# A two-layer graph network: the second layer's gathers without a bound on their indices

## The chip, the cores and the metric

The kernel runs on one core of a Trainium2 chip. The metric is the time of one execution on the device in microseconds (us), as the median of several runs. The engines are named as in the profile: PE is the matrix engine (PEld its weight loads), DVE the vector engine, ACT the scalar engine, POOL is GpSimd and SP the engine that issues most plain transfers.

## The reference

There are 6250 nodes with 256 features, and 106250 edges, sorted by their destination, each with one of 8 types. The first layer sums, for each node, the features of its neighbours and multiplies:

```
x = layernorm(x + relu(x @ w0 + segment_sum((x @ w1)[src_of_message], receiver)))
```

The second layer is an attention over the same edges. For each of the 8 types there is a table `h_all[type] = x @ W[type].T` of 256 features, seen as 8 heads of 32:

```
h_src  = h_all[edge_type, src];  h_dst = h_all[edge_type, dst]
scores = leaky(sum(h_src * attn_src) + sum(h_dst * attn_dst))      # per edge and head, slope 0.2
w      = exp(scores - segment_max(scores, dst));  w = w / segment_sum(w, dst)
x      = layernorm(x + segment_sum(h_src * w, dst))
```

The heavy irregular read is `h_all[edge_type, src]`: one row for every edge, out of 8 x 6250 rows.

## The kernel before, in words

The whole kernel is one function, `graph_layers`, with one block of instructions per engine. All order between the engines is written by hand with semaphores: `x.wait_ge(s, n)` holds an engine until semaphore `s` has reached `n`, and `.then_inc(s, k)` adds `k` when an instruction or a transfer is done. A transfer adds 16 to its semaphore.

The edges are cut into 880 steps. A step holds up to 128 edges (one on each partition) of one tile of 128 destination nodes. Sixteen steps are a batch, and there are 55 batches (NB in the code; B is 16).

First layer (lines 975 to 993): POOL scatters the sums of each step into one of four tables in DRAM with an indirect transfer that adds (line 985, 880 of them). Each carries the bound `node_bound`. Its loop over the batches is a loop on the device. Before it, seven indirect transfers at line 968 fetch rows of edges, also with a bound.

Building of the tables: PE makes the 8 products of each tile of nodes, and ACT writes them with the attention terms to `ha_d` in DRAM, 51200 rows of 264 numbers (256 features and 8 terms, one for each head).

Second layer: for batch b, POOL's `gather(b, s)` (lines 1019 to 1027) issues 16 indirect transfers. Each fetches 128 rows of `ha_d`, picked by the 128 indices in one column of `idx_t`, into one of the 16 places of the buffer `rows[s]`. There are four such buffers, s = b mod 4 (they lie in the memory called `region`). A quarter of four gathers is issued once PE has read the same quarter of that buffer four batches before (`g.wait_ge(segs, ...)`, line 1021). The 880 gathers are written out one by one, as is all of the second layer on PE, DVE and ACT; SP runs a loop.

In iteration i of the layer the engines work on three batches at once: they prepare batch i + 1 (PE line 1361, DVE lines 614 and 619, ACT line 1148), they compute the scores and weights of batch i (DVE line 672 is the first to read the gathered rows of a batch; then DVE lines 674 to 736, PE lines 1392, 1400 and 1412), and they sum batch i - 1: DVE's line 624 multiplies the rows by their weights, a quarter at a time, PE's line 1370 (`sum_edges`) sums the edges of each step into PSUM, which also gives the quarter of the buffer back to POOL, and DVE's line 636 adds the sums to the accumulators.

After the last batch the accumulators are divided by the sums of the weights, the residual is added and the rows are normalised and stored.

The bound of the gathers, `row_bound`, is a register that is set once (line 972) to the last row of the table; an index above it would be an error. The indices all lie within the table.

Of the kernel before, what the change touches and what calls it, by code (L numbers as in the profile page):

```python
# [21 lines left out]
def graph_layers(nc, x, xT, src, dst, etype, w0, w1, W, WT, attn_src, attn_dst, out):  # L22
# [18 lines left out]
    B = P // H  # L41
# [29 lines left out]
    with ExitStack() as ctx:  # L71
        def sb(name, shape, dt):
            return ctx.enter_context(nc.sbuf_tensor(name, shape, dt))

        def sem(name):
            return ctx.enter_context(nc.semaphore(name))
# [9 lines left out]
        idx_t = sb("idx_t", [P, KP], I32)  # L86
# [189 lines left out]
        gath = [[sem(f"gath{s}{q}") for q in range(4)] for s in range(4)]  # L276
# [22 lines left out]
        def in_pairs(eng, first, end, body):  # L299

            with eng.Fori(0, (end - first) // 2) as i:
                for n in range(first, first + 2):
                    body(2 * i + n, n % 2, i + n // 2)
            if (end - first) % 2:
                body(end - 1, (end - 1) % 2, (end - 1) // 2)
# [654 lines left out]
        @block.gpsimd  # L960
        def _(g):
            g.iota(it_i, [[1, P]], base=0, channel_multiplier=0).then_inc(iotas, 1)
            g.iota(pt_i, [[0, 1]], base=0, channel_multiplier=1).then_inc(iotas, 1)

            g.wait_ge(setup, SU["tiles"])
            g.wait_ge(rows_stored, 16)
            for b in range(BLK):
                g.indirect_dma_start(step_f[:, b, :], None, edge_rows_d,
                                     bass.IndirectOffsetOnAxis(ap=i_i[:, b:b + 1], axis=0),
                                     bounds_check=KP - 1, oob_is_err=True).then_inc(step_rows, 16)  # L970
            node_bound = g.snap(g.to_reg(NP_ - 1))
            row_bound = g.snap(g.to_reg(NP_ * R - 1))


            def scatter(it):
                for q in range(4):
                    h = q % 2
                    g.wait_ge(sums_copied, 4 * it + q + 3)
                    g.wait_ge(slots_ready, 4 * it + q + 1)
                    for u in range(4):  # L980

                        if not isinstance(it, int) or q:
                            g.wait_ge(scattered[1 - h][u], 16 * (2 * it + (q + 1) // 2))
                        g.sem_inc(pool_turns, 1)
                        g.indirect_dma_start(sums_d[u],  # L985
                                             bass.IndirectOffsetOnAxis(ap=idx_slot[:, 0, 4 * q + u:4 * q + u + 1], axis=0),
                                             sums[h][:, u, :], None, bounds_check=node_bound, oob_is_err=True,
                                             compute_op=ALU.add).then_inc(scattered[h][u], 16)

            g.wait_ge(zeroed, 16 * NACC)  # L990
            scatter(0)
            with g.Fori(1, ITS) as it:
                scatter(it)

            def add_parts(it, par, turns):
                two = parts[par][:, 2:4, :, :]
                g.wait_ge(parts_in[par], 16 * NACC * (turns + 1))
                g.tensor_tensor(two[:, 0, :, :], two[:, 0, :, :], two[:, 1, :, :], ALU.add).then_inc(pooled, 1)  # L1000

            def inverse_deviation(it, par):
                g.wait_ge(veps_made, it + 1)
                g.tensor_tensor(rstd[par][:, :], veps[par][:, :], minus_half[:, :], ALU.pow).then_inc(rstd_made, 1)  # L1004

            def add_and_invert(it, par, turns):
                add_parts(it, par, turns)
                inverse_deviation(it - 1, 1 - par)

            add_parts(0, 0, 0)  # L1010
            in_pairs(g, 1, ITN, add_and_invert)
            inverse_deviation(ITN - 1, (ITN - 1) % 2)


            for h in range(2):
                g.wait_ge(h_stored[h], 16 * (ITN + 1))
            ha_rows = ha_d.rearrange("n (r w) -> (n r) w", w=AW)

            def gather(b, s):
                for q in range(4):  # L1020
                    g.wait_ge(segs, B * b + 4 * q + 4)
                    g.sem_inc(pool_turns, 1)
                    for u in range(4):
                        k = 4 * q + u
                        g.indirect_dma_start(rows[s][:, k, :], None, ha_rows,  # L1025
                                             bass.IndirectOffsetOnAxis(ap=idx_t[:, B * b + k:B * b + k + 1], axis=0),
                                             bounds_check=row_bound, oob_is_err=True).then_inc(gath[s][q], 16)

            g.wait_ge(begun, 1)
            for b in range(NB):  # L1030
                gather(b, b % 4)


            def finish(it, par, turns):
                g.wait_ge(fveps_made, it + 1)
                g.tensor_tensor(rstd[par][:, :], veps[par][:, :], minus_half[:, :], ALU.pow).then_inc(frstd_made, 1)

            in_pairs(g, 0, ITN, finish)
# [400 lines left out]
```

## Time and profile before

| | |
|---|---|
| median of 3 runs | 3920.17 us (3910.32 to 3921.48) |
| profiled execution | 3891.99 us |
| its span | 3890.1 us |
| its mean TensorE clock, share of the full one | 0.758 |
| POOL busy | 2379.8 us, 61% of the span |
| PE busy | 2260.3 us, 58% |
| DVE busy | 1898.7 us, 49% |
| ACT busy | 1099.7 us, 28% |

The busy shares are averages over stages that differ much: POOL is the fullest engine of the first layer, and PE and DVE are the fullest of the second. The profiled execution is one run, and its time lies below the three others. A row of the trace names the engine, the line of the kernel, the instruction and what it writes and reads (`region<-ha_d,idx_t` is a gather). Where it shows idle time before an instruction it names who ended it; "issue" is time in which the profile shows nothing that the engine waited for, and "another core or an unknown queue" (also "remote") a release of which it shows no source.

### The profile page before, as it was taken

What the parts mean: (1) busy time and instruction counts of PE and PEld (TensorE: products, weight loads), DVE (VectorE), ACT (ScalarE), POOL (GpSimd) and SP (SyncE); (2) the same over time, 40 slices, a digit from 0 to 9 for tenths busy, and PEclk for the clock granted to TensorE, in tenths of its full rate; (3) what the DMA queues carried; (4) which work ended last, traced back from release to release, by engine and by line L of the source; (5) the groups of instructions that cost most, each with busy time, mean ns of one, the idle gap of its engine ahead of it and who ended that gap; (6) DMA issues with size and microseconds to landing.
All of it is one profiled execution on the core that took longest, in us unless ns stands there. A gap on an engine that the chain in (4) does not pass through costs nothing.

```text
span 3890.1 us, 43658 instructions
## 1 busy us (share of the span) xinstructions
PE 2260.3 (58%) x8426; PEld 1550.0 (40%) x8427; DVE 1898.7 (49%) x6684; ACT 1099.7 (28%) x2537; POOL 2379.8 (61%) x1848
## 2 busy tenths in 40 slices
PE   5444444444444444444999926777776676777660
PEld 4333333333333333332555514555545444555440
DVE  2433333333333333332333315777776676777677
ACT  2211222122212221221333303344444333444330
POOL 0477888888888888885111065666666665666601
PEclk8766676666666766676999957888888887888875
DMA  9678876777776767677656433333333333333303
GB/s 339 137 99 136 150 88 88 88 88 88 88 89 88 88 87 88 88 88 165 222 217 227 174 110 82 94 92 98 94 93 93 95 93 89 96 96 96 93 23 114
DMA packets 318535, 443.64 MB, mean 114 GB/s; under 512 B 49188, under 2 KB 273642, under 8 KB 311504
## 3 DMA queue, kind: packets, MB, share of 16 engines
q0 software_dynamic: 169520, 236.24, 38.2%
q1 hardware_dynamic: 141696, 152.01, 13.4%
q10 hardware_dynamic: 7200, 54.07, 3.4%
q8 instruction: 43, 0.70, 0.1%
q14 instruction: 76, 0.62, 0.1%
HBM read 216.80 MB, written 218.81 MB: 112 GB/s over the span
## 4 chain that ended last, share of the span: by engine, by line
issue 31%; PE 29%; DMA 19%; DVE 9%; ACT 5%; POOL 4%; DVEq 1%; another core or an unknown queue 1%; POOLq 0%; ACTq 0%; SPq 0%; PEldq 0%
PE ps L1370 12%; DMA sums_d<-edge_z,idx_slot 11%; PE ps L1315 9%; DMA sums_d<-sums,idx_slot 7%; POOL sums_d L985 4%; PE ps L1361 3%; DVE nodes L636 3%; DVE region L624 2%; ACT edge_z L1083 2%; DVE region L614 1%; PE ps L1223 1%; ACT sums L1083 1%; PE ps L1295 1%; ACT region L1159 1%; DVE region L619 1%
## 5 line engine op out<-in xcount | busy, mean ns | idle before, releaser
L1025 POOL DMA_INDIRECT region<-ha_d,idx_t x880 | 920.5, 1046 | 567.6 <-issue 329.3
L1266 PE MATMUL ps<-region,edge_z 128*128 x1760 | 649.6, 533 | 653.6 <-ACT edge_z L1091 642.4
L1370 PE MATMUL ps<-region 128*128 128x264 f32 x1760 | 681.8, 533 | 375.2 <-DVE nodes L636 236.3
L985 POOL DMA_INDIRECT sums_d<-sums,idx_slot x440 | 689.3, 1567 | 240.6 <-issue 109.6
L985 POOL DMA_INDIRECT sums_d<-edge_z,idx_slot x440 | 686.4, 1560 | 143.9 <-issue 120.1
L1266 PEld LDWEIGHTS ps<-region,edge_z 128*128 128x128 f32 x1760 | 455.2, 272 | 774.9 <-issue 688.4
L1370 PEld LDWEIGHTS ps<-region 128*128 128x128 f32 x1760 | 385.4, 248 | 604.4 <-issue 381.3
L439 DVE TENSOR_TENSOR idx_slot<-dup,edge_z 128x4 int32<-128x4 f32 x220 | 35.9, 163 | 968.8 <-DMA sums_d<-edge_z,idx_slot 512.8
L636 DVE TENSOR_TENSOR nodes<-ps,nodes 128x264 f32 x880 | 378.7, 430 | 141.3 <-DVE nodes L636 68.2
L1315 PE MATMUL ps<-region,edge_z 128*128 128x512 f32 x800 | 351.6, 593 | 0.0
L1361 PEld LDWEIGHTS ps<-edge_z,region 128*128 128x128 f32 x1760 | 276.7, 229 | 80.1 <-issue 62.2
L1083 ACT COPY edge_z<-ps 128x1024 f32<-128x1024 f32 x110 | 111.3, 1012 | 693.9 <-DMA sums_d<-edge_z,idx_slot 693.4
L1361 PE MATMUL ps<-edge_z,region 128*128 x1760 | 263.8, 303 | 53.7 <-issue 52.1
L624 DVE TENSOR_TENSOR region<-region 128x1024 f32<-128x1024 f32 x220 | 266.3, 1211 | 58.0 <-issue 56.1
L1083 ACT COPY sums<-ps 128x1024 f32<-128x1024 f32 x110 | 111.3, 1012 | 638.4 <-DMA sums_d<-sums,idx_slot 618.0
L1152 ACT ACTIVATE region<-iota_row,local_t 128x128 f32<-128x128 f32 x880 | 280.6, 395 | 0.0
L1277 PE MATMUL ps<-edge_z 128*128 128x128 bf16 x880 | 117.1, 276 | 279.7 <-DVE edge_z L423 277.6
L1148 ACT ACTIVATE region<-ps 128x512 f32<-128x512 f32 x220 | 129.9, 590 | 329.2 <-PE ps L1351 205.9
L1277 PEld LDWEIGHTS ps<-edge_z 128*128 128x128 bf16 x880 | 82.2, 126 | 352.2 <-DVE edge_z L423 312.9
L1004 POOL TENSOR_TENSOR rstd<-veps,minus_half 128x2 f32<-128x2 f32 x25 | 23.8, 950 | 320.9 <-DVE veps L583 320.9
L1315 PEld LDWEIGHTS ps<-region,edge_z 128*128 128x128 f32 x800 | 148.4, 191 | 167.2 <-issue 167.2
L614 DVE TENSOR_TENSOR region<-ps,region 128x256 f32<-128x256 f32 x220 | 92.9, 422 | 242.4 <-PE ps L1361 143.0
(173 smaller groups left out, 2567.5 us busy)
## 6 DMA issues: line engine op xcount, KB each, us to landing
ha_d<-region ACTq DMA_DIRECT2D x50, 1056.0 KB, 4.0
row<-step_rows_d SPq DMA_DIRECT2D x220, 128.0 KB
sums_d<-sums SPq DMA_DIRECT2D x4, 6400.0 KB, 28.8
region<-sums_d SPq DMA_DIRECT2D x100, 256.0 KB, 3.7
region<-ha_d,idx_t POOLq DMA_INDIRECT x880
edge_z<-level_d SPq DMA_DIRECT2D x55, 136.0 KB
kl_d<-nodes SPq DMA_DIRECT2D x8, 903.0 KB
edge_z<-kl_d SPq DMA_DIRECT2D x55, 129.0 KB
```

The costliest lines, as they stand in the source:

```text
L614: v.tensor_tensor(prod[q % 2], ps[:, 5 + q % 2, 0:4 * RH] .rearrange("p (u h r) -> p u h r", u=4, h=H), tmask[s % 2][:, 4 * q:4 * q + 4, : ...
L624: v.tensor_tensor(rows[s][:, 4 * q:4 * q + 4, 0:D].rearrange("p u (h d) -> p u h d", h=H), rows[s][:, 4 * q:4 * q + 4, 0:D].rearrange("p u ...
L636: v.tensor_tensor(acc[:, ds(tile[u] * AW, AW)], ps[:, u, 0:AW], acc[:, ds(tile[u] * AW, AW)], ALU.add).then_inc(added, 1)
L985: g.indirect_dma_start(sums_d[u], bass.IndirectOffsetOnAxis(ap=idx_slot[:, 0, 4 * q + u:4 * q + u + 1], axis=0), sums[h][:, u, :], None, b ...
L1025: g.indirect_dma_start(rows[s][:, k, :], None, ha_rows, bass.IndirectOffsetOnAxis(ap=idx_t[:, B * b + k:B * b + k + 1], axis=0), bounds_ch ...
L1083: a.copy(sums[h][:, :, :], ps[:, 2 + 2 * h:4 + 2 * h, :].rearrange("p b (u n) -> p (b u) n", u=2)).then_inc(sums_copied, 1)
L1152: last = a.activation(apart[q % 2][:, u, :], iota_row[:, :], ACT.Abs, bias=local_t[:, ds(B * b + 4 * q + u, 1)], scale=-1.0)
L1266: mm = t.matmul(ps[:, 2 + 2 * h + u // 2, (u % 2) * D:(u % 2) * D + D], lhsT=counts[h][:, u, :], rhs=y_sb[:, ds(tile[4 * q + u] * D, D)], ...
L1277: mm = t.matmul(ps[:, h, u * P:(u + 1) * P], lhsT=onehot[h][:, u, :], rhs=eq[h][:, u, :], start=True, stop=True)
L1315: mm = t.matmul(ps[:, 4 + q, :], lhsT=xts[par][:, h, c, :], rhs=wT_sb[:, c, 512 * q:512 * q + 512], start=(c == 0), stop=(c == DC - 1))
L1361: mm = t.matmul(ps[:, 5 + q % 2, RH * u:RH * u + RH], lhsT=st[q % 2][:, u, :], rhs=b_sb[:, ds(tile[4 * q + u] * RH, RH)], start=True, stop ...
L1370: t.matmul(ps[:, u, 0:AW], lhsT=sel[q][:, u, :], rhs=rows[s][:, 4 * q + u, :], start=True, stop=True).then_inc(segs, 1)
```

## The change

The gathers of the second layer lose two arguments, the bound and what is to happen beyond it. The scatters of the first layer and the transfers of line 968 keep theirs. The register `row_bound` is still set, and nothing reads it.

```
                         g.indirect_dma_start(rows[s][:, k, :], None, ha_rows,
-                                             bass.IndirectOffsetOnAxis(ap=idx_t[:, B * b + k:B * b + k + 1], axis=0),
-                                             bounds_check=row_bound, oob_is_err=True).then_inc(gath[s][q], 16)
+                                             bass.IndirectOffsetOnAxis(ap=idx_t[:, B * b + k:B * b + k + 1],
+                                                                       axis=0)).then_inc(gath[s][q], 16)
```

## Rows read from the trace of the kernel before

**Rows 1.** Busy us (instructions) of PE, PEld, DVE, ACT, POOL; then clock, DMA share, GB/s.

```profile
2350.00:3800.00 1450.00, 1010.13 (x4099) 716.61 (x4099) 1039.34 (x2714) 574.49 (x1626) 858.99 (x821) 0.82 0.34 89
```

**Rows 2.** The chain that ended last, its shares by line.

```profile
PE ps L1370 12%; DMA sums_d<-edge_z,idx_slot 11%; PE ps L1315 9%; DMA sums_d<-sums,idx_slot 7%; POOL sums_d L985 4%; PE ps L1361 3%; DVE nodes L636 3%; DVE region L624 2%; ACT edge_z L1083 2%; DVE region L614 1%; PE ps L1223 1%; ACT sums L1083 1%; PE ps L1295 1%; ACT region L1159 1%; DVE region L619 1%
```

**Rows 3.** Line 1025: busy, mean ns, idle before; ns min/median/max; who waited for it.

```profile
L1025 POOL DMA_INDIRECT region<-ha_d,idx_t x880 | 920.5, 1046 | 567.6 <-issue 329.3 <-PE ps L1370 226.9 <-remote 11.4
...
L1025 POOL DMA_INDIRECT region<-ha_d,idx_t x880: 1006/1012/2055, 2257.7 to 3692.9; - x176
...
  DVE region L672: 8.3, 1
```

**Rows 4.** Line 1025 in two stretches: ns min/median/max, first and last start.

```profile
L1025 POOL DMA_INDIRECT region<-ha_d,idx_t x64: 1007/1012/1133, 2257.7 to 2340.9; - x64
...
L1025 POOL DMA_INDIRECT region<-ha_d,idx_t x272: 1006/1012/2008, 2355.7 to 2797.4; - x136
```

**Rows 5.** DVE's line 672, once a batch: start us, us.

```profile
2351.27 0.28 DVE L672 TENSOR_TENSOR region<-region 128x128 f32<-128x128 f32 x1
...
2800.26 0.28 DVE L672 TENSOR_TENSOR region<-region 128x128 f32<-128x128 f32 x1
...
3639.95 0.28 DVE L672 TENSOR_TENSOR region<-region 128x128 f32<-128x128 f32 x1
3665.64 0.28 DVE L672 TENSOR_TENSOR region<-region 128x128 f32<-128x128 f32 x1
3694.92 0.29 DVE L672 TENSOR_TENSOR region<-region 128x128 f32<-128x128 f32 x1
3720.30 0.28 DVE L672 TENSOR_TENSOR region<-region 128x128 f32<-128x128 f32 x1
3746.03 0.28 DVE L672 TENSOR_TENSOR region<-region 128x128 f32<-128x128 f32 x1
```

**Rows 6.** Timeline of POOL within a batch; in brackets the idle time before.

```profile
2805.78 1.01 POOL L1025 DMA_INDIRECT region<-ha_d,idx_t  x1 [0.30 <-issue]
```

**Rows 7.** Line 985, the scatters: ns min/median/max.

```profile
L985 POOL DMA_INDIRECT sums_d<-sums,idx_slot x440: 1552/1553/2180, 137.3 to 1798.2; - x147
```

**Rows 8.** Busy time, columns as in rows 1, after the last gather.

```profile
3697.00:3723.00 26.00, 19.42 (x84) 13.76 (x84) 19.33 (x54) 11.44 (x34) 0.00 (x0) 0.85 0.12 32
```

**Rows 9.** A gather beside DVE's line 624, and that line's durations.

```profile
3690.50 1.23 DVE L624 TENSOR_TENSOR region<-region 128x1024 f32<-128x1024 f32 x1 [1.05 <-issue]
3690.55 2.06 POOL L1025 DMA_INDIRECT region<-ha_d,idx_t  x1 [0.30 <-issue]
...
L624 DVE TENSOR_TENSOR region<-region x220: 1191/1215/1247, 2349.7 to 3773.0; 128x1024 f32<-128x1024 f32 x110
```

**Rows 10.** Timeline of the first 92 us of the second layer.

```profile
2257.70 1.13 POOL L1025 DMA_INDIRECT region<-ha_d,idx_t  x1 [51.94 <-issue]
...
2280.64 0.29 DVE L672 TENSOR_TENSOR region<-region 128x128 f32<-128x128 f32 x1 [8.27 <-DMA region<-ha_d,idx_t]
...
2286.47 0.64 PE L1351 MATMUL ps<-region,nfeat 128*128 128x512 bf16 x1
...
2311.30 0.42 DVE L614 TENSOR_TENSOR region<-ps,region 128x256 f32<-128x256 f32 x1 [17.02 <-issue]
...
2314.11 0.60 ACT L1148 ACTIVATE region<-ps 128x512 f32<-128x512 f32 x1 [21.28 <-remote]
...
2335.80 0.42 DVE L614 TENSOR_TENSOR region<-ps,region 128x256 f32<-128x256 f32 x1 [22.30 <-issue]
...
2349.72 1.23 DVE L624 TENSOR_TENSOR region<-region 128x1024 f32<-128x1024 f32 x1 [0.95 <-issue]
```

**Rows 11.** The chain of waits in the same stretch, in order of time.

```profile
2294.28 17.02 issue
```

**Rows 12.** Timeline of ACT: its longest waits in the steady part.

```profile
2396.79 0.60 ACT L1148 ACTIVATE region<-ps 128x512 f32<-128x512 f32 x1 [5.86 <-remote]
...
3213.54 0.60 ACT L1148 ACTIVATE region<-ps 128x512 f32<-128x512 f32 x1 [6.66 <-remote]
```

## The prediction

> **What bounds the kernel now.** I read the busy time by stage first. The stages are: preparation to about 137 us; the first layer, in which GpSimd scatters, to about 1810 us; the building of the tables to 2250 us; the second layer with its gathers, to about 3783 us; the last normalisation. The changed line works in the second layer alone. In the steady part of it, 2350 to 3800 us, PE is busy 1010 us of 1450, DVE 1039 and POOL 859, so POOL is not the fullest engine, and the DMA engines stand at 0.34 [rows 1]. A busy share does not say who is waited for, so the chain of waits comes next: over the whole run PE's line 1370 has 12% of it, the scatters' transfers 18%, and line 1025 is not among its lines at all [rows 2]. Third, the view of line 1025 itself: 880 gathers, nearly all at 1.006 to 1.012 us, with 227 us of POOL's idle time spent waiting for PE's line 1370, the instruction that gives a buffer back. In the other direction one engine waited for a gather once in the whole run: DVE's line 672, for 8.3 us [rows 3].
>
> How far ahead the gathers run can be counted. Four buffers of 16 gathers form the ring. 64 + 272 = 336 gathers, 21 batches (0 to 20), have started by 2797.4 us [rows 4]. DVE reads batch 1 at 2351.27, batch 18 at 2800.26 and batch 52 at 3694.92 [rows 5], a period of (3694.92 - 2351.27)/51 = 26.35 us. So when DVE reads batch 18 the gathers of 20 are out and those of 21 begin, to be read three periods, some 78 us, later. POOL needs 16 x (1.046 busy + 0.30 of issue) = 21.5 us of each 26.35 us [rows 3, 6]. It has 4.8 us over in each batch, 0.30 us a gather.
>
> **The change part by part.** One thing is removed: the operand that holds the bound, from 880 gathers. The scatters of line 985 and the seven gathers of line 968 keep theirs, so nothing before 2250 us can move. No instruction, wait, transfer or byte is added or moved, and the indices are all within the table. What remains is how long POOL takes over one gather.
>
> (a) *The price of one gather.* Every indirect transfer in the trace carries a bound, so the price of the check is not in a row and is bounded from both sides. A gather takes 1.012 us for 128 rows, 7.9 ns a row, and a scatter that adds takes 1.553 us [rows 4, 7]. The 0.54 us between them is the most that any option of such an instruction is seen to cost here. I bound the check by it in both directions: 0.54 us less, or 0.54 us more if the form without a bound is worked off in another way. I take 0.10 us less. It is one comparison beside the reading of an index, the forming of an address and the writing of what the DMA engines work from, and a tenth of the nearest row, the gather's 1.012, is a fair share for it. POOL's period goes from 1.316 to 1.216 us in a burst.
>
> (b) *The steady part: 816 gathers.* 816 x 0.10 = 82 us less work on POOL. The work beside it is the batch of PE and DVE, 26.35 us long. POOL's spare time grows from 4.8 to 6.4 us a batch and goes into its wait for PE's line 1370, since the buffer comes no earlier. The trace holds a test of this: the last gather starts at 3692.9 us [rows 3], and the batches after it run with POOL idle. The batch with 16 gathers from 3639.95 takes 25.69 us; the ones without take 25.38 (from 3694.92) and 25.73 (from 3720.30) [rows 5, 8]. So even taking the gathers away altogether moves a batch by -0.31 to +0.04 us; a tenth of one less moves nothing. Value 0; end of the range 0.31 x 0.1 x 51 = 1.6 us of gain. If the cover were gone, each 0.1 us a gather would be worth 16 x 0.1 x 51 = 82 us.
>
> Gathers and DVE do touch each other in one direction: the gather that starts at 3690.55, 0.05 us after DVE's line 624, takes 2.06 instead of 1.01 us, while line 624 itself, 220 times, never leaves 1.191 to 1.247 us [rows 9]. The Trainium skill ("SBUF — State Buffer", on the shared port pair) says that a VectorE instruction with two inputs in SBUF and a GpSimd instruction that reads SBUF exclude each other, and that whichever starts second is held until the first ends. The stretched gather agrees with it. The other direction, DVE held by a gather, would be worth something here; it is rival E.
>
> (c) *The head of the layer: 16 gathers.* POOL starts at 2257.70 and DVE's line 672 starts at 2280.64, after 8.27 us of waiting for the sixteenth gather [rows 10]. This is on the path: 16 x 0.10 = 1.6 us of gain. Bounds: at 0.54 less, 8.27 us (the wait is then gone and line 672 follows line 619); at 0.54 more, 8.6 us of loss.
>
> (d) *The rest of the first burst: 48 gathers.* From 2278 to 2342 us POOL issues batches 1 to 3 without a pause, and the other engines stand nearly still: DVE's line 614 starts at 2311.30 after 17.02 us and at 2335.80 after 22.30 us, and ACT's line 1148 at 2314.11, although the PE product it needs is recorded at 2286.47. The chain calls the first of them "issue" [rows 10, 11], which names nobody. DVE's first line 624 comes at 2349.72, after the last gather of the burst (2340.9 + 1.0) [rows 4], and from there on all is regular. Whether the burst holds the others or merely lies beside them the trace does not say. As neither end of a stall lies on the end of a batch of gathers (2278.6, 2299.7, 2320.7, 2341.8 by 1.316 us each), I take 0. The other end is 48 x 0.10 = 4.8 us of gain, or 26 at 0.54.
>
> **The sum.** Against the profiled execution, 3891.99 us (its span of 3890.1 and 1.9 around it): 0 (b) - 1.6 (c) - 0 (d) = -1.6, so 3890.4. The median of the runs shown is 3920.17, 0.7% above the profiled one, and I scale: 3890.4 x 3920.17/3891.99 = 3918.5, given as 3918.
>
> **The rivals.**
> *A, the burst sets the ramp.* If the other engines are held until POOL's first 64 gathers are out, the saving is 64 times the saving of one: 6.4 us at 0.10 (3914), 12.8 at 0.2 (3907), 35 at 0.54 (3885). For it: all engines idle while POOL is at its densest, and return to the regular beat 8 us after it stops. Against it: stretches that end inside the burst, and that in the steady part runs of 16 gathers go by with only rare holds. It passes 0.3% (11.8 us, about what can be told from no change here) from 0.18 us a gather.
>
> *B, slower: the form without a bound is longer, and POOL becomes the engine that a batch waits for.* The place is line 1025 in the steady part. It decides from 0.30 us a gather more, the spare time found above. At 0.40 more a batch of gathers takes 27.9 us, (27.9 - 26.35) x 51 = 79 us of loss and 6 more at the head, 4005 us; at 0.54 more, 30.2 us a batch, 196 + 9 us, 4125. For it only that no row shows this form; against it that it is the same instruction with an operand less.
>
> *E, faster: gathers hold DVE's starts.* A DVE instruction held back would start late and keep its length, so its length clears nobody. If each of the four instructions of line 624 in a batch waited out the rest of a gather, 0.10 us less of each gather would give back at most 4 x 0.10 x 51 = 20 us, 3898. This is the second half of the skill's rule on the shared port pair. Against it stand the two batches without gathers, of which one is no faster than the one with them [rows 5].
>
> *C, no difference.* The bound is compared in any case, or its cost is too small to see: 3920 us. For it: the gap of 0.30 us between two indirect transfers and their flat durations, 1.006 to 1.012, which look like a fixed path.
>
> *D, slower: denser bursts lengthen PE's holds.* Three times in the steady part, first at 2396.79 and last at 3213.54, ACT's line 1148 waited 5.9 to 6.7 us for a PE that the profile shows waiting for nothing, each time amid gathers [rows 12]. A gather of 128 x 1056 bytes every 1.216 us is 111 GB/s instead of 103 within a burst. If such holds became two or three more, 12 to 18 us would go: 3932 to 3938. They are too few for more.
>
> **How the numbers follow.** Forecast 0.45, C 0.20, A 0.20, E 0.02, B 0.05, D 0.08. Of A, 0.15 lies beyond 0.3%, and E does; the scatter of the runs (3910.32 to 3921.48) gives faster 0.03 more from the others. Faster 0.20. Slower: B 0.05, D 0.05, scatter 0.02, so 0.12. Within 0.3%: 0.68. The forecast's own range is 3907 to 3928, the spread of the runs around it. The range at 8 in 10 goes down to 3896 for A up to 0.35 us a gather (22 us, and some scatter) and up to 3932 for the near end of D; B is left out.
>
> **What would show it.** (a) Line 1025's median in the changed kernel: about 0.91 us; 1.01 means C, over 1.3 means B. (b) The period of DVE's line 672 stays at 26.3 us, and POOL's wait for PE's line 1370 grows from 227 us towards 300. A shorter period would make me wrong about the cover. (c) The wait of line 672 falls from 8.3 to about 6.7 us. (d) From the start of the first gather to the first line 624 it was 2349.72 - 2257.70 = 92.0 us; about 90.4 is right, 86 or less by the saving of 64 gathers is A. Before 2250 us nothing changes. The prediction is wrong if the time leaves 0.3%, or if it stays and the steady part and ramp have both moved against each other.

## The result, and the profile after

| | before | after |
|---|---|---|
| median of 20 runs each | 3906.38 us (3882.77 to 3921.82) | 3931.45 us (3919.00 to 3950.12) |
| ratio, 95% interval | | 1.0070 (1.0052 to 1.0089) |
| profiled execution | 3891.99 us | 3939.08 us |
| its span, its clock | 3890.1 us, 0.758 | 3937.3 us, 0.761 |

The kernel became slower, by 0.7%. The profiled execution of before is near the fast end of its runs and that of after above the middle of its own, so the two traces lie further apart (47.1 us) than the medians (25.1 us). Of the 47.1 us, 7.6 lie before the first gather (2257.7 against 2265.3), where nothing is changed; they are scatter, not an effect of the change (in e5, the same kernel, the first gather starts at 2257.7).

The view of line 1025 and its first 64 gathers, against [rows 3, 4]:

```profile
L1025 POOL DMA_INDIRECT region<-ha_d,idx_t x880: 940/946/1957, 2265.3 to 3739.2; - x176
its engine sat idle before it (us, times) until:
  issue: 332.3, 766
  PE ps L1370: 304.3, 104
...
L1025 POOL DMA_INDIRECT region<-ha_d,idx_t x64: 942/946/1101, 2265.3 to 2344.4; - x64
```

A gather costs 0.946 us instead of 1.012, and its gap stays at 0.30: one every 1.25 us instead of 1.316. POOL's wait for PE's line 1370 grew from 227 to 304 us. Both are what a hidden saving looks like. But the last gather starts at 3739.2 instead of 3692.9 us: the layer itself is longer. DVE's line 672, the beat of the batches, against [rows 5]:

```profile
2292.52 0.29 DVE L672 TENSOR_TENSOR region<-region 128x128 f32<-128x128 f32 x1
...
2363.24 0.28 DVE L672 TENSOR_TENSOR region<-region 128x128 f32<-128x128 f32 x1
...
3741.27 0.29 DVE L672 TENSOR_TENSOR region<-region 128x128 f32<-128x128 f32 x1
3767.25 0.28 DVE L672 TENSOR_TENSOR region<-region 128x128 f32<-128x128 f32 x1
3793.15 0.28 DVE L672 TENSOR_TENSOR region<-region 128x128 f32<-128x128 f32 x1
```

Three numbers come from these rows and serve below: from the first gather to batch 0 27.2 us (before 22.9); from batch 0 to batch 1, the head, 70.7 (before 70.6); from batch 1 to 54 a mean period of (3793.15 - 2363.24)/53 = 26.98 us (before 26.32 by the same count). The period alone is 53 x 0.66 = 35 us. Busy times do not explain it; the columns are those of [rows 1]:

```profile
2350.00:3800.00 1450.00, 995.60 (x3999) 722.50 (x4069) 1009.25 (x2631) 572.43 (x1618) 807.08 (x816) 0.81 0.34 88
```

In a window of the same length DVE does a little less (1009 us instead of 1039) and the clock is 0.81 where it was 0.82. PE's numbers can't be compared closely: the trace of after has records of only 148 of the 220 products of line 1351, that of before of all 220. What grew is a wait. ACT's line 1148, from 2350 to 3790 us, first of after, then of before (busy, mean ns of one, idle before it and who ended it):

```profile
L1148 ACT ACTIVATE region<-ps 128x512 f32<-128x512 f32 x214 | 126.5, 591 | 327.6 <-remote 152.8 <-PE ps L1351 127.3 <-PE ps L1361 25.1
```

```profile
L1148 ACT ACTIVATE region<-ps 128x512 f32<-128x512 f32 x211 | 124.5, 590 | 258.9 <-PE ps L1351 186.6 <-remote 54.1 <-issue 14.7
```

ACT's idle time before this line grew from 258.9 to 327.6 us (21.3 us of the latter still belong to the head, which ends later in this trace). "Remote" is a release without a recorded source, and it went from 54 to 153 us, but the name alone proves nothing: where the record of a product is missing, an ordinary wait of 2 us for it is called remote too. Length does tell. From batch 1 on this line waits longer than 3.3 us 7 times before (35.8 us in all) and 30 times after (122.1 us), whatever the name. One of them in the timeline of after, against the two of [rows 12]:

```profile
2963.92 0.38 PE L1351 MATMUL ps<-region,nfeat 128*128 128x512 bf16 x1
2964.08 1.01 POOL L1025 DMA_INDIRECT region<-ha_d,idx_t  x1 [0.50 <-issue]
...
2964.43 0.60 ACT L1148 ACTIVATE region<-ps 128x512 f32<-128x512 f32 x1 [2.28 <-PE ps L1351]
...
2965.40 0.95 POOL L1025 DMA_INDIRECT region<-ha_d,idx_t  x1 [0.30 <-issue]
...
2966.65 0.95 POOL L1025 DMA_INDIRECT region<-ha_d,idx_t  x1 [0.30 <-issue]
...
2969.30 0.38 PE L1351 MATMUL ps<-region,nfeat 128*128 128x512 bf16 x1
2969.63 1.08 POOL L1025 DMA_INDIRECT region<-ha_d,idx_t  x1 [0.62 <-issue]
...
2971.01 0.95 POOL L1025 DMA_INDIRECT region<-ha_d,idx_t  x1 [0.30 <-issue]
2972.26 0.95 POOL L1025 DMA_INDIRECT region<-ha_d,idx_t  x1 [0.30 <-issue]
2973.52 0.95 POOL L1025 DMA_INDIRECT region<-ha_d,idx_t  x1 [0.30 <-issue]
2974.57 0.42 DVE L614 TENSOR_TENSOR region<-ps,region 128x256 f32<-128x256 f32 x1 [4.40 <-remote]
...
2975.91 3.14 PEld L1370 LDWEIGHTS ps<-region 128*128 128x128 f32 x8 [6.57 <-issue]
...
2975.99 0.60 ACT L1148 ACTIVATE region<-ps 128x512 f32<-128x512 f32 x1 [7.44 <-remote]
```

The first product of line 1351 ends at 2964.30 and ACT reads it at 2964.43, 0.13 us later. The second ends at 2969.68 and ACT reads it at 2975.99, 6.3 us later; DVE and PE stand still with it, POOL's gathers go on. I call such a stretch a hold. The tables below count holds by ACT's waits above 3.3 us, on any line, that the profile calls remote, from batch 1 on: 7 in before (35.8 us in all), 22 in after (98.2 us). As the 30 waits above show, this count is a low one.

### The profile page after: what moved, and what is told of

It is laid out like the page before. It is cut to its first block, busy times and chain, and to the rows that moved or that the text cites. A ratio compares the mean times of both kernels' runs of the same rounds, so it can differ in the third digit from the quotient of the medians.

```text
span 3937.3 us, 43584 instructions
## 1 busy us (share of the span) xinstructions
PE 2253.3 (57%) x8354; PEld 1558.4 (40%) x8427; DVE 1905.9 (48%) x6684; ACT 1100.2 (28%) x2537; POOL 2327.2 (59%) x1848
## 4 chain that ended last, share of the span: by engine, by line
issue 31%; PE 30%; DMA 19%; DVE 6%; ACT 6%; POOL 4%; another core or an unknown queue 2%; DVEq 1%; POOLq 0%; ACTq 0%; SPq 0%
PE ps L1370 13%; DMA sums_d<-edge_z,idx_slot 11%; PE ps L1315 9%; DMA sums_d<-sums,idx_slot 7%; PE ps L1361 4%; POOL sums_d L985 3%; ACT edge_z L1083 2%; DVE nodes L636 2%; PE ps L1223 1%; DVE region L624 1%; ACT sums L1083 1%; DVE region L614 1%; ACT region L1152 1%; PE ps L1295 1%
## 5 line engine op out<-in xcount | busy, mean ns | idle before, releaser
L1025 POOL DMA_INDIRECT region<-ha_d,idx_t x880 | 867.9, 986 | 658.8 <-issue 332.3
L1361 PE MATMUL ps<-edge_z,region 128*128 x1760 | 270.3, 307 | 70.6 <-ACT region L1148 36.7
```

Source lines behind the costliest of these rows:

```text
L1025: g.indirect_dma_start(rows[s][:, k, :], None, ha_rows, bass.IndirectOffsetOnAxis(ap=idx_t[:, B * b + k:B * b + k + 1], axis=0)).then_inc( ...
L1361: mm = t.matmul(ps[:, 5 + q % 2, RH * u:RH * u + RH], lhsT=st[q % 2][:, u, :], rhs=b_sb[:, ds(tile[4 * q + u] * RH, RH)], start=True, stop ...
```

## The experiments

Each run is set against the kernel before on the same chip. The chips turned out to be of two kinds: on some the kernel before has a median of 3888 to 3906 us and the traces have holds, on the others 3805 to 3810 us, and in no trace of any kernel there does ACT have a single remote wait in the second layer after batch 0. "With holds" and "without holds" below mean this. One chip was used twice, some 50 minutes apart (for e5 to e8 and for e16), and had holds both times; the others of these experiments were used once, so that this belongs to the chip and not to the hour is likely but not shown. "Start, head, period" are the three numbers defined above (us).

### Alone, or with a small pause behind each gather: without holds

```
+                        g.wait_ge(paused, B * b + k)
+                        g.memset(pause[:, :], 0.0).then_inc(paused, 1)     # 128x1, behind every gather
```

Here e1 has the gathers without a bound and e2 with it; e3 drops the bound only where `b < 4`, e4 only where `b >= 4`, and both have no pause.

> The changed kernel with one small memset on POOL (128x1, its own tile) behind each of the 880 gathers, which should cost about 0.1 us and bring the gathers back to the bounded pace of 1.32 us or a little slower. Theory PACE (a faster burst of gathers makes PE's holds more frequent): the loss of 0.7% goes, ratio to before 0.998 to 1.002, mean batch period 26.3 us. Theory FORM (what is fetched without a bound is itself the burden, whatever its pace): stays at 1.005 to 1.009, period about 27.0. Theory HEAD (the loss lies in the first 92 us of the layer): the head returns to 92 us from 98.

> The kernel before with the same memset behind each of its bounded gathers, pace about 1.42 us in place of 1.32. Theory PACE, carried on: holds become rarer still, ratio 0.993 to 0.999. Theory FORM: nothing moves, 0.998 to 1.003, since POOL has 0.30 us a gather to spare and the pause takes about 0.1. If the pause itself costs (POOL becomes late), over 1.003.

> Only the gathers of batches 0 to 3 (the first burst of 64) lose their bound, the other 816 keep it. Theory HEAD: the whole loss is here, 1.005 to 1.009. Theories PACE and FORM in the steady part: 0.998 to 1.002, at most a few us of gain from the shorter head.

> The 816 gathers from batch 4 on lose their bound, the first 64 keep it. Theory HEAD: 0.998 to 1.002. Theories PACE and FORM: 1.004 to 1.009, mean batch period about 27.0 us against 26.3.

| | ratio to before (3809.75 us) | start, head, period |
|---|---|---|
| e1 | 0.9994 (0.9985 to 1.0003) | 21.9, 21.0, 25.60 |
| e2 | 0.9999 (0.9990 to 1.0008) | 22.9, 21.5, 25.60 |
| e3 | 0.9996 (0.9987 to 1.0005) | 21.9, 21.0, 25.62 |
| e4 | 0.9999 (0.9990 to 1.0008) | 23.0, 21.3, 25.61 |

The expectations name their theories: PACE (what hurts is how densely the gathers follow each other), FORM (what hurts is the form without a bound, at any pace), HEAD (the loss lies in the first 92 us). Nothing here is slower, so nothing here can tell them apart, and e3 and e4, made to split the loss between head and steady part, have no loss to split: that split rests on the traces above alone. It showed something else: the head is 21 us and not 71, and the period 25.6, the same for both forms. The timeline of e4 in its head, against [rows 10] (its gathers there carry the bound, its lines are 5 higher than in after from the gather on):

```profile
2278.47 0.60 ACT L1153 ACTIVATE region<-ps 128x512 f32<-128x512 f32 x1 [2.89 <-PE ps L1356]
...
2286.90 0.29 DVE L672 TENSOR_TENSOR region<-region 128x128 f32<-128x128 f32 x1 [8.29 <-DMA region<-ha_d,idx_t]
...
2290.21 0.60 ACT L1153 ACTIVATE region<-ps 128x512 f32<-128x512 f32 x1 [1.86 <-PE ps L1356]
...
2308.23 0.29 DVE L672 TENSOR_TENSOR region<-region 128x128 f32<-128x128 f32 x1 [5.31 <-DMA region<-ha_d,idx_t]
```

ACT never waits for an unknown release, and batch 1 begins 21.3 us after batch 0, when its sixteenth gather lands. The time to batch 0, 22.9 us with the bound and 21.9 without, differs by 16 x 0.066 = 1.06 us: step (c), at the true price. The small pause of 0.11 us fell into the gap of 0.30 us and left the cadence as it was.

### The same on a chip with holds, and the gathers taken away

```
-                        v.wait_ge(gath[s][q], 64 * (t + 1))                # e7
+                        v.wait_ge(gath[s][q], 64)
...
+                        if b < 4:                                          # e7: gathers with their bound
...
-                        g.indirect_dma_start(rows[s][:, k, :], None, ha_rows,
+                        wide = AW if b < 4 else H                          # e8: 8 numbers of a row, no bound
+                        g.indirect_dma_start(rows[s][:, k, 0:wide], None, ha_rows if b < 4 else ha_narrow,
```

The lines removed here are those of after. e7 leaves out the 816 gathers of batch 4 and later, bound and all, and works on the rows that lie in the buffers; POOL's waits for PE all stay. e5 is the changed kernel again, e6 is the kernel of e1.

> The changed kernel unaltered, beside the kernel before on one chip. The kernel before took 3906 us where the change was first timed and 3810 us beside the last four kernels, and in the traces of the latter DVE and ACT wait nowhere long for PE: the holds are missing. Theory HOLDS (the change costs only where PE's holds occur, by making more of them): if before takes about 3810 here, ratio 0.999 to 1.001; if about 3900, 1.004 to 1.009. Theory EVERYWHERE (the whole change costs on any chip, and the partial ones hid it): 1.004 to 1.009 also at 3810.

> The gathers without a bound, each with the small memset behind it, once more. With before at about 3900 us (holds present), PACE: 0.998 to 1.002, FORM: 1.004 to 1.009. With before at about 3810 us it tells nothing new, 0.998 to 1.001.

> The kernel before with the 816 gathers of batch 4 and later left out; the batches work on the rows that lie in the buffers. It leaves out most of the second layer's data. With holds present, if the gathers cause those of the steady part: mean batch period 25.5 to 25.7 us and some 35 us less time (0.990 to 0.992); if the holds come from elsewhere: 26.3 us, 0.998 to 1.001. Without holds: at most 0.1 us a batch less, 0.998 to 1.000; if POOL or the gathers' transfers were what a batch waits for after all, more than 1% less.

> The changed kernel with each gather from batch 4 on fetching 8 numbers a row in place of 264 (32 bytes in place of 1056), as many descriptors, the same 880 instructions on POOL. It leaves out most of the second layer's data. With holds present: if the bytes cause them they go (0.990 to 0.993), if POOL's instructions or the count of descriptors do they stay as in the changed kernel (1.004 to 1.009). Without holds: 0.998 to 1.001, line 1025 at 0.94 to 0.95 us as before.

| | ratio to before (3889.08 us) | start, head, period | waits above 3.3 us |
|---|---|---|---|
| e5 | 1.0097 (1.0060 to 1.0133) | 27.3, 70.7, 27.02 | 29, 123.7 us |
| e6 | 1.0116 (1.0080 to 1.0152) | 36.4, 50.8, 27.25 | 29, 127.3 us |
| e7 | 0.9909 (0.9878 to 0.9940) | 22.9, 70.9, 25.64 | none |
| e8 | 1.0104 (1.0057 to 1.0151) | 25.8, 72.3, 26.88 | 21, 92.2 us |

e5 repeats the result. e6 came out on the side of FORM (1.004 to 1.009 expected, 0.998 to 1.002 for PACE), but it is no test: its memset left the gathers at 1.25 us in a run. e7 is the telling one: without the 816 steady gathers the period falls to the 25.6 us of the chips without holds, and the long waits are gone, while the head, which keeps its 64 gathers, is as before. Batches 0, 1 and 54, and ACT's line 1148 (here 1149) from 2350 to 3790 us:

```profile
2278.99 0.29 DVE L672 TENSOR_TENSOR region<-region 128x128 f32<-128x128 f32 x1 [6.97 <-DMA region<-ha_d,idx_t]
...
2349.86 0.28 DVE L672 TENSOR_TENSOR region<-region 128x128 f32<-128x128 f32 x1
...
3708.71 0.28 DVE L672 TENSOR_TENSOR region<-region 128x128 f32<-128x128 f32 x1
```

```profile
L1149 ACT ACTIVATE region<-ps 128x512 f32<-128x512 f32 x211 | 124.4, 590 | 216.5 <-PE ps L1352 144.1 <-remote 72.4
```

The 72.4 us of "remote" are in short waits, none above 2.5 us; 148 of 220 products have a record here too. The head's timeline:

```profile
2281.62 0.63 PE L1352 MATMUL ps<-region,nfeat 128*128 128x512 bf16 x1
2282.29 0.60 ACT L1149 ACTIVATE region<-ps 128x512 f32<-128x512 f32 x1 [1.86 <-PE ps L1352]
...
2312.00 0.60 ACT L1149 ACTIVATE region<-ps 128x512 f32<-128x512 f32 x1 [20.65 <-remote]
...
2337.19 0.60 ACT L1149 ACTIVATE region<-ps 128x512 f32<-128x512 f32 x1 [24.50 <-remote]
```

So the holds need gathers in flight, and POOL's waits for PE, which e7 keeps, don't make them alone. In the head POOL waits for nobody between its 64 gathers, and it has the longest holds of all. e8 moves 32 bytes a row instead of 1056, loses as much time as after and has about as many holds: the bytes are not the cause.

Which gathers hold? I took each product of line 1351 from batch 1 to the last gather that has a record and for which ACT stood idle, and called it late if ACT read it more than 1 us after its end. Beside it I put its place in the run: how many gathers POOL had started by then in a row. A run goes on as long as the next gather starts within 2.2 us of the last, so a stretched gather or a short wait for PE does not end it:

| gathers in the run | before, mostly every 1.316 us | after, mostly every 1.25 us | e5, mostly every 1.25 us |
|---|---|---|---|
| 1 | 0 late of 29 | 0 of 19 | 0 of 20 |
| 5 | 0 of 46 | 13 of 35 | 21 of 34 |
| 8 | 1 of 10 | 1 of 10 | 3 of 13 |
| 9 | 11 of 21 | 6 of 7 | 3 of 3 |

With the bound the fifth gather of a run never comes with a late product, without it in 34 of 69 cases. This is a pattern and not yet a rule. The eighth place is out of line (4 of 23 without the bound), and if any gap over 0.35 us ends a run, late products stand at its first gather too, 10 of 89 before and 19 of 58 after.

In the head the last hold ends 90.1 us after the first gather with the bound and 88.5 without, 1.41 and 1.38 us for each of the 64 gathers. That suggests a backlog: something that takes 1.4 us a gather and falls behind by 0.08 us with each gather at 1.316 us and by 0.15 at 1.25. The steady part does not bear it out. With each gather's actual start and 1.4 us for each, the backlog is 0.9 to 1.2 us at 37 products of before, none late, and at 25 of after, 10 late; one threshold doesn't serve both. Two things are shown: the holds need gathers (e7) and not their bytes (e8). That the cadence made more of them in after, rather than the form of the instruction, isn't.

### Pauses long enough to change the cadence, and longer runs: without holds

e9, e10 and e13 have the pause of e1 with another tile, e11 and e12 (repeated as e14 and e15) one wait for PE in a batch instead of four:

```
+        pause = sb("pause", [P, 336], BF16)      # e9 no bound, e10 bound; e13: [P, 112], no bound
...
+                g.wait_ge(segs, B * b + B)       # e11, e14 bound; e12, e15 no bound
-                    g.wait_ge(segs, B * b + 4 * q + 4)
```

> The short pause did not slow the gathers: its memset fitted into the 0.30 us between two of them (cadence 1.25 us with it and without). Here the memset is 128x336 bf16, about 0.4 us, for a cadence of some 1.32 to 1.40 us with unbounded gathers. Where holds are present (before near 3890 to 3910 us): PACE gives 1.000 to 1.003 and a mean batch period of 26.0 to 26.4 us; FORM gives 1.006 to 1.012 and 27.0. Where they are absent (before near 3810): 0.999 to 1.001.

> The kernel before with the same long memset behind each gather, cadence about 1.40 us. With holds: PACE gives fewer of them, 0.991 to 0.997, a period under 26.2 us; FORM gives 0.999 to 1.002 and 26.3. If POOL becomes too slow (over 1.60 us a gather) the time rises. Without holds 0.999 to 1.001.

> Bounded gathers, but POOL waits once a batch for the whole buffer and then issues 16 in one run, instead of waiting before every four. If what hurts is the length of an unbroken run of gathers (theory RUN), holds increase: 1.004 to 1.015. If what hurts is that POOL waits and wakes often (theory WAKE: the unbounded form only makes POOL reach its wait sooner, 304 to 336 us of waiting against 227), holds decrease: 0.990 to 0.998. Without holds 0.999 to 1.001.

> The same single wait a batch with gathers without a bound. With holds: WAKE gives a time near that of the bounded kernel with one wait, under 1.000; RUN and FORM give more than the changed kernel's 1.010, or as much. Without holds 0.999 to 1.001.

> Gathers without a bound with a memset of 128x112 bf16 behind each, about 0.20 us. Between the long memset and the next gather 0.17 us passed, so the cadence should be 0.95 + 0.20 + 0.17 = 1.32 us, that of the kernel before. Where holds are present (before at 3890 to 3910 us): PACE 0.998 to 1.003 and a batch period of 26.2 to 26.4 us; FORM 1.006 to 1.012 and 27.0. Where they are absent (before near 3805): 0.999 to 1.001.

> Bounded gathers with one wait a batch, once more, for a comparison where holds are present. RUN (the length of an unbroken run of gathers): 1.004 to 1.015. WAKE (how often POOL waits for PE's semaphore and wakes): 0.990 to 0.998. PACE says nothing of it. Without holds 0.999 to 1.001, as measured.

> Gathers without a bound with one wait a batch. With holds: WAKE gives under 1.000 and within 0.003 of the bounded kernel with one wait; PACE and FORM give 0.004 to 0.010 over that kernel; RUN gives over 1.010. Without holds 0.999 to 1.001, as measured.

| | ratio to before (3804.6 us) | a gather every | start, head, period |
|---|---|---|---|
| e9 | 1.0023 (1.0013 to 1.0032) | 1.51 us | 25.7, 24.6, 25.67 |
| e10 | 1.0214 (1.0198 to 1.0230) | 1.58 us | 26.8, 25.3, 26.86 |
| e11, e14 | 0.9994 (0.9985 to 1.0003), 0.9997 (0.9988 to 1.0006) | 1.32 us | 22.9, 21.3, 25.58 to 25.61 |
| e12, e15 | 0.9992 (0.9983 to 1.0002), 0.9997 (0.9988 to 1.0006) | 1.25 us | 21.8 to 22.0, 21.0, 25.59 to 25.62 |
| e13 | 1.0001 (0.9992 to 1.0010) | 1.32 us | 23.0, 21.3, 25.63 |

All seven ran on chips without holds. So whether longer runs (RUN in the expectations) or the number of POOL's waits for PE (WAKE) make more holds is not settled, and e13, which has the unbounded gathers at before's pace and would have told PACE from FORM, could not do so. e9 and e10 came out slower than expected (0.999 to 1.001). Two things are settled. On these chips runs of sixteen gathers at 1.25 us cost nothing. And the cover of step (b) is real and near the size that the prediction gave it (0.30 us a gather; with the period of these chips it is (25.6 - 21.5)/16 = 0.26). At 1.51 us, 0.19 more than before, the period moves by 0.07 us; at 1.58, 0.26 more, POOL is the bound, and 16 x 1.58 = 25.3 us, and gathers stretched to as much as 2.03 us, make 26.86. The view of e10's gathers names who waits now:

```profile
L1027 POOL DMA_INDIRECT region<-ha_d,idx_t x880: 1017/1018/2027, 2257.6 to 3729.3; - x176
...
  PE ps L1374: 3.1, 19
who waited for it (us, times):
  DVE region L674: 55.5, 25
```

### The unbounded gathers slowed down on chips with holds

```
+                    g.wait_ge(paused, 4 * b + q + 1)                       # before each four gathers
+                    n = 4 if b < 4 else 2                                  # e17; e16, e18: always 4
+                    g.tensor_tensor(pause[:, 1, 0:n], pause[:, 0, 0:n], pause[:, 0, 0:n], ALU.pow).then_inc(paused, 1)
```

> Gathers without a bound, with one POOL instruction (a power of a 128x4 tile of ones, about 1 us) before each group of four, so that four gathers take about 6.0 us in place of 5.0 and 1.25 us becomes 1.5 on average. From the traces with holds: PE is late only after at least 9 gathers in a row at 1.32 us, or at least 5 at 1.25 us, and the first 64 gathers end in a last hold 1.38 to 1.41 us per gather after their start, as if something took each gather in 1.4 us. Where holds are present (before at 3890 to 3910 us), theory DRAIN (PACE with that number): no long holds at all, the head 45 to 50 us shorter and the batches 0.7 us shorter than before's 26.3, ratio 0.978 to 0.985. FORM: 1.006 to 1.012. Where they are absent (before near 3805): 1.000 to 1.004.

> As the last kernel, but the pause is shorter (128x2, about 0.7 us) from batch 4 on, since with 1.04 us before every four gathers POOL had only 7 us left to wait in all and the batch took 26.18 us. Four gathers then take about 5.7 us, 1.42 each. DRAIN, with holds present: no or few holds, head about 25 us, period 25.6 to 25.8, ratio 0.978 to 0.984. If 1.4 us is too little margin, some holds come back: 0.984 to 0.990. With holds absent: 0.999 to 1.001.

> The kernel of the last run once more, beside the one with shorter pauses. With holds present 0.985 to 0.991 as before. With holds absent the cover is thin: the head is 5 us longer and the batches are at POOL's 25.6 to 26.2 us, 1.001 to 1.010.

| | ratio to before | median, before | start, head, period | waits above 3.3 us |
|---|---|---|---|---|
| e16 | 0.9881 (0.9842 to 0.9920) | 3842.33, 3888.13 us | 24.9, 24.6, 26.18 | none |
| e17 | 0.9814 (0.9785 to 0.9844) | 3822.36, 3893.70 us | 25.0, 24.6, 25.88 | 5, 17.0 us |
| e18 | 0.9873 (0.9846 to 0.9899) | 3845.43, 3893.70 us | 25.0, 24.5, 26.31 | none |

The gathers are still without a bound and still come at 1.25 us within a four; with the pause, four take at least 6.04 us (e16) or 5.69 us (e17), 1.51 and 1.42 a gather, against 4.98 to 5.0 in a run of after. e17 in its timeline (with batches 0, 1 and 54) and in the view of its gathers:

```profile
2280.33 0.29 DVE L674 TENSOR_TENSOR region<-region 128x128 f32<-128x128 f32 x1 [10.76 <-DMA region<-ha_d,idx_t]
...
2304.93 0.29 DVE L674 TENSOR_TENSOR region<-region 128x128 f32<-128x128 f32 x1 [8.59 <-DMA region<-ha_d,idx_t]
...
3676.68 0.28 DVE L674 TENSOR_TENSOR region<-region 128x128 f32<-128x128 f32 x1
```

```profile
2959.79 0.95 POOL L1030 DMA_INDIRECT region<-ha_d,idx_t  x1 [0.30 <-issue]
...
2962.30 0.95 POOL L1030 DMA_INDIRECT region<-ha_d,idx_t  x1 [0.30 <-issue]
...
2963.27 1.63 POOL L1027 TENSOR_TENSOR pause<-pause 128x2 f32<-128x2 f32 x1
...
2964.39 0.60 ACT L1154 ACTIVATE region<-ps 128x512 f32<-128x512 f32 x1 [2.15 <-PE ps L1357]
...
2965.10 1.00 POOL L1030 DMA_INDIRECT region<-ha_d,idx_t  x1 [0.20 <-issue]
```

```profile
L1030 POOL DMA_INDIRECT region<-ha_d,idx_t x880: 942/957/1940, 2255.3 to 3642.9; - x176
...
  PE ps L1376: 5.9, 30
who waited for it (us, times):
  DVE region L674: 19.4, 2
```

POOL is busy without a break here (it waits for PE 5.9 us in all), and yet the last gather starts at 3642.9 us instead of 3692.9. In e16 no product of line 1351 in 101 is late, in e17 3 of 86. So the form without a bound does not hold the others at any pace, as FORM had it (1.006 to 1.012), and spacing the gathers takes the holds away, those that the kernel before had too. It is not their mean rate: over the steady part four gathers take 6.73 us on the mean in after and 6.33 in e17, which issues more of them in the same time and holds less. What is left open is that the pause also ends nearly all of POOL's waits for PE (7.1 us in e16, 304 in after), and that the pause is an instruction of its own; the head, where POOL has no such wait in any kernel, speaks for the spacing. The head, 70.6 us in the kernel before, falls to 24.6: 46 us, and the change moved none of them. The steady part gives 53 x (26.32 - 25.88) = 23 us in e17; with the 2 us that batch 0 begins later the sum is 67 us, and the medians are 71 apart. In e16 POOL is so nearly the bound that DVE waited for gathers 21 times (40.5 us), which the shorter pause mends:

```profile
  DVE region L674: 40.5, 21
```

Of the expectations with holds present (0.978 to 0.985 for e16, where DRAIN is the backlog as a theory, 0.978 to 0.984 for e17, 0.985 to 0.991 for e18) the first missed by 0.003, the other two were met. e17 is the fastest version on a chip with holds, 1.9% faster than the kernel before. Its price on a chip without them was not measured; e9, with a similar mean cadence, lost 0.2% there. Nor was the bound put back under these pauses.

## Why the prediction was wrong

The prediction said 3918 us and no difference; the time went up by 25 us. The step that failed is (b), "816 steady gathers, value 0", together with rival D's "too few for more": the batch grew from 26.32 to 26.98 us, 35 us over 53 batches.

- **(a) Right in kind, 0.066 us instead of 0.10.** The bound is part of the gather's duration, and the gap of 0.30 us does not hide it.
- **(b) Wrong where there are holds, right elsewhere.** The cover of 0.30 us a gather is there, and on chips without holds e4 measured 0.9999. But it weighs only the time that POOL saves, not what the gathers do to the other engines' waits. My test of it compared a batch of 25.69 us with gathers with 25.38 and 25.73 without. That batch had no hold in it. The mean period was 26.32, and the mean without gathers is 25.64 (e7): the gathers cost 0.68 us a batch already, 36 us, and the change doubled this. With gathers and without holds the batch is 25.58 to 25.63 us, no longer than without gathers, so on the chips with holds the 36 us belong to the holds (the traces of before and e7 are from different chips; beside each other on one chip the medians differ by 33.7 us). The test should have used the mean of all batches with gathers.
- **(c) Right in mechanism.** 16 x 0.066 = 1.0 us, seen as 22.9 against 21.9 us on chips without holds. Under holds batch 0 came at 27.2 us, and the gain was lost in them. The 8.27 us wait for the sixteenth gather, on which I based it, is gone in after: line 614 is held until 2291.50, after that gather, and line 672 follows it.
- **(d) The value was near, the reason was not.** The head is 70.6 against 70.7 us, so the bound moved nothing in it; from the first gather to the first line 624 it took 96.4 us where I expected 90.4 and before had 92.0; 4.3 of the 4.4 us more than before lie ahead of batch 0. But I left open whether the stall is the burst's doing. It is: it goes when the gathers are spaced out (e16), and it is 46 to 50 us long (70.6 against 24.6 in e16 and 21 without holds).
- **Rival D was the case in its outcome**: more holds. That denser bursts make them is its reason; the runs agree with it but don't separate it from the form of the instruction. I priced it at two or three holds more, 12 to 18 us; there were 15 more by the low count above, and 35 us in the profiled run. With eyes on the three waits above 5 us I had left out those of 4 us, and I did not ask at what length of a run the holds begin, which the rows of before could answer.
- **B** came true in no run of the change, but its threshold of 0.30 us is borne out by e10. **C** falls with the duration. **A** was right that the burst holds the others and wrong on the price: the last hold ends 1.6 us earlier after the first gather, not 64 x 0.066 = 4.2, and the head as a whole is no shorter. **E** had no run of its own, but with gathers and without holds the batch takes 25.58 to 25.63 us, without gathers 25.64, so there is nothing that it could give.

What stays open: what it is that holds back releases while gathers are in flight, why some chips show none of it, whether the shorter gather makes more holds by its cadence or by its form, and whether longer runs (e11, e12) would make it worse where it exists.

## What to carry to other kernels

An engine with time to spare can still cost the others time by what it issues meanwhile, so cover by spare time is a bound on what a saving gives, not on what it takes. Where a profile shows unusually long waits amid bursts of indirect transfers, compare the mean period with and without bursts over many batches, and go by the length of the waits and not by the name "remote", which a missing record gives to ordinary waits too; then try to space the transfers, before making them cheaper. Compare only against runs of the old kernel on the same chip.

## What the runs showed of the hardware

- A bound on the indices of an indirect gather of 128 rows costs 0.066 us of 1.012. The width of the rows hardly matters: a gather without a bound takes 0.944 us in e8, nearly all with rows of 32 bytes, and 0.946 in after, with 1056.
- On some chips, runs of such gathers at 1.25 to 1.32 us each go with waits of ACT of 3.3 to 24.5 us for products that PE had long recorded as done or that have no record; with a pause before each four, 1.42 to 1.51 us a gather, waits above 3.3 us of this kind are nearly gone (5 in e17, none in e16 and e18). On others even runs of more than 64 leave no trace. The kernel before is 78 to 102 us (2.0 to 2.6%) faster there.
- A memset of 128x1 (0.11 us) behind a gather fits into the 0.30 us gap: the next gather starts 1.25 us after the last, as without it.
